# Bank order of the token stages, the third attention's second half and the last stage in a two-layer transformer kernel

## What is computed

```
x = x + g_msa * self_attn(ln(x) * (1 + sc) + sh)             # windows
x = x + g_mca * topk_cross_attn(ln(x) * (1 + sc) + sh, ctx)  # 16 of 154 keys
x = x + g_mlp * (silu(a) * b @ w_m2)                         # SwiGLU
x = x + mha(ln1(x), ln1(x)) + t_sa                           # 1024 keys
x = x + mha(ln3(x), ctx, mask) + t_ca
x = x + gelu(ln2(x) @ w1 + b1) @ w2 + t_mlp
```

## Time and profile before

| | |
|---|---|
| median of 3 runs | 1565.24 us (1562.11 to 1566.72) |
| profiled execution, its own time | 1565.28 us |
| its span in the profile | 1563.5 us |
| mean granted TensorE clock | 0.96 of full |
| PE busy | 1395.5 us, 89% of the span |
| DVE busy | 918.0 us, 59% |
| ACT busy | 716.2 us, 46% |
| POOL busy | 341.6 us, 22% |

### The profile page before, as it was taken

One profiled execution on the slowest core, in us unless ns is written; L12 is line 12 of the kernel. 1 busy time (PEld: TensorE's weight loads), 2 busy tenths in 40 slices (PEclk: granted clock), 3 DMA queues, 4 the chain that ended last, 5 costly groups with the idle time before them and its releaser, 6 DMA issues.

```text
span 1563.5 us, 25438 instructions
## 1 busy us (share of the span) xinstructions
PE 1395.5 (89%) x9100; PEld 681.9 (44%) x9100; DVE 918.0 (59%) x2815; ACT 716.2 (46%) x1454; POOL 341.6 (22%) x377
## 2 busy tenths in 40 slices
PE   7999776879889796889899999999999989987898
PEld 5467554444544452342224333333333334543576
DVE  3556397988877785755465666667576235640220
ACT  2255454555465363115544565555455654543221
...
PEclk9999988789989898989999999999999999999999
...
DMA packets 22092, 26.74 MB, mean 17 GB/s; under 512 B 4204, under 2 KB 19634, under 8 KB 21708
## 3 DMA queue, kind: packets, MB, share of 16 engines
...
...
## 4 chain that ended last, share of the span: by engine, by line
PE 75%; DVE 10%; ACT 6%; issue 5%; POOL 3%; DMA 1%; SPq 0%; ACTq 0%; POOLq 0%; DVEq 0%
PE bank L1022 27%; PE bank L979 10%; PE bank L1062 8%; PE bank L994 7%; PE bank L958 5%; PE bank L937 3%; PE bank L916 2%; PE bank L964 2%; PE bank L1105 1%; DVE x_hat L1441 1%; PE bank L1086 1%; PE bank L944 1%; DVE left L1496 1%; DVE left L1503 1%; ACT pr L1252 1%
## 5 line engine op out<-in xcount | busy, mean ns | idle before, releaser
L1252 ACT ACTIVATE pr<-bank 128x512 f32<-128x512 f32 x656 | 355.0, 597 | 295.8 <-PE bank L1022 291.7
L1468 DVE TENSOR_REDUCE part_max<-bank 128x1 f32<-128x512 f32 x512 | 327.4, 684 | 210.8 <-PE bank L1022 209.8
L1022 PE MATMUL bank<-slot 32*128 32x512 f32 (+1 forms) x3072 | 398.5, 522 | 10.0 <-ACT pr L1252 5.6
L1022 PEld LDWEIGHTS bank<-slot 32*128 32x128 f32 x3072 | 157.6, 185 | 230.5 <-issue 168.6
L1518 POOL TENSOR_SCALAR var_eps<-mean_var 128x4 f32<-128x4 f32 x24 | 5.5, 230 | 966.1 <-DVE mean_var L1432 966.1
L1574 POOL TENSOR_SCALAR left<-left 128x308 f32<-128x308 f32 x128 | 125.2, 978 | 105.0 <-ACT exp_all L1274 45.3
L979 PE MATMUL bank<-h_t,w_m 128*128 128x512 f32 x256 | 130.8, 635 | 11.9 <-ACT hidden L1228 4.7
L1062 PE MATMUL bank<-pr,v 128*17 128x512 f32 x1024 | 135.6, 601 | 0.0
L1576 POOL TENSOR_TENSOR probs<-left,exp_all 128x308 f32<-128x308 f32 x128 | 107.1, 837 | 10.6
L1493 DVE MAX8 top<-bank 128x8 f32<-128x154 f32 x256 | 69.3, 311 | 42.2 <-PE bank L1086 31.9
L1274 ACT ACTIVATE exp_all<-bank,neg 128x154 f32<-128x154 f32 x256 | 85.5, 386 | 10.1 <-DVE left L1496 5.9
...
## 6 DMA issues: line engine op xcount, KB each, us to landing
...
```

What stands on the lines that cost most here:

```text
L1022: last = nc.tensor.matmul(g.bank(*tile)[:, into], left, right, start=True, stop=True)
L1252: nc.scalar.activation(m.pr[:, u % NPR, :], g.bank("s", gi, i)[:, :], ACT.Exp).then_inc(g.free("s", gi, i), 1)
L1468: nc.vector.tensor_reduce(m.part_max[:, slot, h * TB + i // 8, i // 4 % 2:i // 4 % 2 + 1], bank[:, :], axis=AX.X, op=ALU.max).then_inc(don ...
```

## The change

It changes `banks_of`, `own_bank`, the choice of the bank in `finish`, the second half of the third attention in `group_run`, the maxima of group 24 in `last_run`, and where stage (6, 0) lies in `make_plan`.

- In the third attention from round 161 (of -4 to 287) to round 251 the same 364 tiles are written in rounds of four and three in turn: two s and two m, two s and one m, two s and two m, one s and two m. They may take all seven banks, 0 to 6, and so may "o_turn" and "m_turn" of groups 22 and 23, the "s" tiles up to the attention's end, and "on_turn", "y_mm", "hat_turn" and "qk" of stage (5, 0). "pv" of a group of four "s" tiles is written a round later than before. 24 token steps and turns lie in this stretch, as before.
- (2, 1), (3, 0), (4, 0) and the "o_turn" of the second attention take their two banks, 0 and 6, in turn; so does the first half of (3, 1) under the first maxima, and those maxima have banks 1 to 5 left.
- Elsewhere a bank of one's own is taken only if it was last filled more than three steps before.
- The "ug" of stage (6, 0) take the seven banks in turn; its head comes earlier, and its first three "ug" stand between the last "pv" and "o_turn" of the fourth attention.
- The first maxima of group 24 are five rounds of three (one of four) and not four of four.

```diff
@@ -56,6 +57,10 @@
 
 ROUNDS = {1: 4, 3: 32}
 LEAD = {1: 2, 3: 4}
+
+
+THREES = 252 - 7 * 13
+FOURS_AND_THREES = ((2, 2), (2, 1), (2, 2), (1, 2))
 M_HEADS_4 = ((0, 2), (0, 3), (0, 0), (0, 1), (1, 2), (1, 3), (2, 0), (2, 1), (2, 2), (2, 3), (1, 0), (1, 1))
 
 
@@ -79,11 +84,22 @@
 RING = ("o_turn", "on_turn", "y_mm", "hat_turn", "qk", "v", "ua", "ub", "ug", "down", "ck", "cv", "ctx_turn", "mcol", "mgate", "mbv", "mtp")
 
 
+def shares_all(step):
+
+    if step[0] in ("m", "s") and attention(step[1]) == 3:
+        return (step[1] - 16 + (step[0] == "s")) * ROUNDS[3] + step[2] // 2 >= THREES + LEAD[3] * (step[0] == "m")
+    if step[0] in ("m_turn", "o_turn"):
+        return 22 <= step[1] < 24
+    return step[0] in ("on_turn", "y_mm", "hat_turn", "qk") and step[1:3] == (5, 0)
+
+
 def banks_of(step):
 
     kind = step[0]
+    if shares_all(step):
+        return (0, 1, 2, 3, 4, 5, 6)
     if kind in ("m", "m_turn", "s"):
-        return (3, 4, 5, 6) if attention(step[1]) == 1 else (1, 2, 3, 4, 5, 6)
+        return (3, 4, 5, 6) if attention(step[1]) == 1 else (1, 2, 3, 4, 5) if kind == "m" and step[1] == 16 else (1, 2, 3, 4, 5, 6)
     if kind == "c_score":
         return (1, 2, 3, 4)
     if kind == "c_turn":
@@ -101,13 +117,24 @@
     s, b = step[1:3]
     if s == 6:
         return (0, 1, 2, 3, 4, 5, 6)
-    early = (s, b) == (3, 1) and (kind == "ua" and step[3:] == (0, 0) or kind == "hat_turn" and step[3] == 0 or kind in ("on_turn", "y_mm") and step[3] < 2)
-    return (0, 6) if early or (s, b) in ((2, 1), (3, 0), (4, 0)) else (0, 1, 2)
+    return (0, 6) if (s, b) in ((2, 1), (3, 0), (4, 0)) or first_maxima(step) else (0, 1, 2)
+
+
+def first_maxima(step):
+
+    kind, (s, b) = step[0], step[1:3]
+    if (s, b) != (3, 1):
+        return False
+    return step[3] == 0 if kind in ("hat_turn", "ua", "ub") else step[3] < 2
 
 
 def own_bank(step):
 
-    return attention(step[1]) > 1 if step[0] == "o_turn" else step[1:3] in ((2, 1), (3, 0), (4, 0), (3, 1), (4, 1), (5, 0), (5, 1), (6, 0))
+    if step[0] == "o_turn":
+        return 16 <= step[1] < 22 or step[1] >= 24
+    if step[1:3] == (6, 0):
+        return step[0] in ("on_turn", "y_mm", "hat_turn")
+    return step[1:3] in ((4, 1), (5, 1)) or step[1:3] == (3, 1) and not first_maxima(step)
 
 
 SOON = ("ck_a", "cv_copy", "x_hat", "on_copy", "modulate", "ua_copy", "silu", "qk_a", "v_copy")
@@ -163,7 +190,8 @@
             if banks:
                 banks = [x for x in banks if x not in last or last[x][0] != "down_part" or ("down",) + last[x][1:4] in placed]
                 empty = [x for x in banks if x not in last or follow_up(last[x]) in placed]
-                first = banks[0] if step[0] in RING and own_bank(step) and banks[0] in empty else None
+                apart = len(self.steps) - turn.get(banks[0], -9) > 3
+                first = banks[0] if step[0] in RING and own_bank(step) and banks[0] in empty and apart else None
                 bank = min(empty or banks, key=lambda x: turn.get(x, -1)) if first is None else first
                 if not empty:
                     follow = follow_up(last[bank])
@@ -327,6 +355,15 @@
     def time(c):
         return start + first * (min(c, turn) + lead) + then * max(c - turn, 0)
 
+    def round_of(t, width, tiles, double=False):
+        if tiles:
+            plan.at(t, *tiles, ("scores", *tiles))
+        plan.at(t + 0.3 * width, *[("m_red",) + x[1:] for x in tiles if x[0] == "m"], *[("exp",) + x[1:] for x in tiles if x[0] == "s"])
+        for x in tiles:
+            last_of[x] = len(begins) + double
+        begins.append(t)
+
+    begins, last_of, stream = [], {}, ([], [])
     for c in range(-lead, 9 * rounds):
         t, width = time(c), time(c + 1) - time(c)
         gs, xs = c // rounds - 1, c % rounds
@@ -338,27 +375,43 @@
             maxima = [("m", gi_m, i) for i in range(2 * xm, 2 * xm + 4)] if xm % 2 == 0 else []
         if gm > 7:
             weighed = [("s", gi_s, i) for i in range(2 * xs, 2 * xs + 4)] if xs % 2 == 0 else []
-        tiles = [x for both in zip(weighed, maxima) for x in both] if len(weighed) == len(maxima) else maxima + weighed
-        if tiles:
-            plan.at(t, *tiles, ("scores", *tiles))
-        plan.at(t + 0.3 * width, *[("m_red",) + x[1:] for x in maxima], *[("exp",) + x[1:] for x in weighed])
+        if a == 3 and THREES <= c < 8 * rounds - lead:
+            stream[0].extend(weighed)
+            stream[1].extend(maxima)
+            while len(stream[0]) + len(stream[1]) >= 7:
+                k = len(begins) - first_three
+                for j in range(2):
+                    n_s, n_m = FOURS_AND_THREES[(k + j) % 4]
+                    tiles = [x for pair in itertools.zip_longest(stream[0][:n_s], stream[1][:n_m]) for x in pair if x]
+                    del stream[0][:n_s], stream[1][:n_m]
+                    round_of(time(THREES + (k + j) * 0.875), width, tiles)
+        else:
+            tiles = [x for both in zip(weighed, maxima) for x in both] if len(weighed) == len(maxima) else maxima + weighed
+            round_of(t, width, tiles, not (weighed and maxima))
+            first_three = len(begins)
         if c % 2:
             gaps[c] = t + 0.6 * width
-        if gm < 8 and xm == rounds - 1:
-            if a == 3:
-                plan.at(t + 0.5 * width, ("m_neg", gi_m))
-                plan.at(time(c + 1) + 0.35 * (time(c + 2) - time(c + 1)), ("m_turn", gi_m), ("m_copy", gi_m), ("max_rows", gi_m))
-            else:
-                plan.at(t + 0.9 * width, ("m_turn", gi_m), ("m_copy", gi_m), ("max_rows", gi_m))
-        if gs >= 0 and xs % per == per - 1:
-            d = xs // per
-            t1, width = time(c + 1), time(c + 2) - time(c + 1)
-            plan.at(t1 + 0.4 * width, ("pv", gi_s, d))
+    assert not stream[0] and not stream[1]
+    for gi in range((a - 1) * 8, a * 8):
+        c = last_of["m", gi, M_UNITS[a] - 1]
+        t, width = begins[c], begins[c + 1] - begins[c]
+        if a == 3:
+            plan.at(t + 0.5 * width, ("m_neg", gi))
+            plan.at(t + 1.35 * width, ("m_turn", gi), ("m_copy", gi), ("max_rows", gi))
+        else:
+            plan.at(t + 0.9 * width, ("m_turn", gi), ("m_copy", gi), ("max_rows", gi))
+        for d in range(PV_STEPS[a]):
+            c = last_of["s", gi, (d + 1) * S_UNITS[a] // PV_STEPS[a] - 1]
+            c += 2 if a == 3 and begins[c] >= time(THREES) and begins[c] < time(8 * rounds - lead) else 1
+            last = c + 1 >= len(begins)
+            t1 = begins[c] if c < len(begins) else begins[-1] + (c + 1 - len(begins)) * then
+            width = then if last else begins[c + 1] - begins[c]
+            plan.at(t1 + 0.4 * width, ("pv", gi, d))
             if (d + 1) % (PV_STEPS[a] // 2) == 0:
                 half = (d + 1) // (PV_STEPS[a] // 2) - 1
-                plan.at(t1 + 0.9 * width, ("o_copy", gi_s, half))
-                plan.at(t1 + 1.5 * width, ("o_turn", gi_s, half))
-                plan.at(t1 + 1.9 * width, ("o_norm", gi_s, half))
+                plan.at(t1 + 0.9 * width, ("o_copy", gi, half))
+                plan.at(t1 + 1.5 * width, ("o_turn", gi, half))
+                plan.at(t1 + 1.9 * width, ("o_norm", gi, half))
     return time(9 * rounds), gaps
 
 
@@ -382,9 +435,9 @@
         plan.at(t + 0.52 * per, ("o_turn", gi, half))
         plan.at(t + 0.6 * per, ("o_norm", gi, half))
 
-    for x, (gi, numbers) in enumerate(((24, (0, 1, 2, 3)), (24, (6, 7, 8, 9)), (24, (4, 5, 10, 11)), (25, (0, 1, 2, 3)))):
+    for x, (gi, numbers) in enumerate(((24, (0, 1, 2)), (24, (6, 8, 3)), (24, (7, 9, 4)), (24, (5, 10, 11)), (25, (0, 1, 2, 3)))):
         scores(early[x], *maxima_in(gi, *numbers))
-    plan.at(early[3] + 0.3 * per, ("m_turn", 24), ("m_copy", 24), ("max_rows", 24))
+    plan.at(early[3] + 0.6 * per, ("m_turn", 24), ("m_copy", 24), ("max_rows", 24))
     for n in range(16):
         gi, half, t = 24 + n // 2, n % 2, start + n * per
         tails, one, two = [("s", gi, 5 * half)], [("s", gi, 5 * half + i) for i in (1, 2)], [("s", gi, 5 * half + i) for i in (3, 4)]
@@ -526,16 +579,17 @@
     plan.at(where[-1] + 0.1, ("load_row", 8), ("load_out", 6))
     R4 = 6.4
     A4 = end + 0.6 * R4
-    end, gaps4 = last_run(plan, A4, R4, [gaps[c] + 0.1 for c in (267, 271, 275, 279)])
+    end, gaps4 = last_run(plan, A4, R4, [gaps[c] + 0.1 for c in (259, 263, 267, 271, 275)])
     five = joined([gap_slots(5, 1, n) for n in range(2)])
     plan.fill(five, [gaps[c] for c in range(277, 288, 2)] + gaps4[:10])
     plan.at(A4 + 7 * R4, ("load_row", 9), ("load_out", 7))
     six = [[block_slots(6, b, n) for n in range(2)] for b in range(2)]
-    plan.fill(six[0][0][0], gaps4[20:31])
-    for (b0, n0), t in (((0, 1), 19), ((1, 0), 49), ((1, 1), 86)):
+    for b0, n0, t in ((0, 0, 0), (0, 1, 19), (1, 0, 49), (1, 1, 86)):
         six[b0][n0][0].append([six[b0][n0][1][0].pop(0) for _ in range(CK)])
-        plan.spread(six[b0][n0][0], end + t, end + t + 16)
```

(5 more changed lines are left out.)

1 line of the change is left out of this document (added).

## The result

The changed kernel took **1521.0 us** (median of 4 runs, 1520.14 to 1521.69) against 1566.0 for the kernel before (4 runs beside it); the ratio is 0.9717, with a 95% interval of 0.9699 to 0.9735. Forecast were 1515 and a range of 1500 to 1543. The medians and ratios of this document leave out three executions that took far longer: one of 3190.8 and one of 3023.6 us, of the first two kernels under the experiments, and one of 1667.1 us of the kernel before. The kernel before took 1563.1 to 1566.0 us beside the different kernels, so small differences between kernels are better read from the ratios. The profiled execution has a span of 1519.4 us against 1563.5, so 44.1 us are to be found. The page first: busy time, share of the span, instructions, and the granted clock in 40 slices.

The account below looks back on a forecast made before the run. PE's queue, busy 89% of the span, was taken to set the end; waits removed, -18 - 19 - 3 - 6 - 2 - 2 = -50, took 1565.3 to 1515 us, range 1500 to 1543.

Parts of the forecast that it names:

- Last stage: Stage (6, 0): "ug" every 1.72 us instead of 2.76; -18 us, bounds -19 and -14 if the head's x_hat is late.
- Third attention, second half: Rounds of four and three on seven banks end PE's bank waits; -19 us, bounds 0 and -27.
- token steps: Third attention's second half: idle 1.54 and 0.69 before "on_turn" go with own banks; -3 us, bounds 0 and -4.
- 3.38 a period against 3.98; over 45 periods 27 us: Third attention's second half: average period after against before, a full gain of 27 us, of which 70% was taken.
- B's wait: Third attention before: half of a period's second round of four tiles waits 0.85 us for a bank.
- The discount of 30%: Third attention's second half: 70% of 27 us taken, for DVE's bursts and 24 token steps and turns sharing the seven banks.
- First maxima: Taking banks 0 and 6 in turn ends most of about 8.5 us idle; -6 us, bounds +1 and -9.
- Second attention: Banks 0 and 6 alternate, order stays; DVE's lateness makes the step behind wait again; -2 us, bounds +2 and -8.
- Group 23 and fourth attention: With group 24's maxima: seventh bank, second "on_turn" or "hat_turn" on another bank; -2 us, bounds +2 and -6.
- Rival 1: Third attention: two tiles of one head in a round cost a turn, losing 22 us; 1537 us, chance 0.12.
- Rival 2: Third attention: ring of weights (eight "exp" slots) or DVE's bursts bind instead of banks; gain 3 of 22, 1534 us, chance 0.13.
- Rival 3: Third attention: a round costs the same whatever it holds, 1.5 us each; slower, 1579 us, chance 0.05.

Follow-up runs that it names:

- the first two kernels under the experiments: Changed kernel with the second attention's token steps and o_turn on their own bank as before, 1517.3 us; kernel before with only "ug" taking its banks in turn, 1547.9 us.
- its mend: Changed kernel with "o_turn" of groups 20 and 21 also on any of seven banks, not held to bank 0: 1516.2 us.
- extra tiles took the room in B: Kernel before, two score tiles computed twice in 43 second rounds (B) of groups 20 to 22, ahead of B's two tiles that wait for a bank: 1578.6 us.

## Why the prediction was right, and where it was not

**Last stage, -18 forecast, -15.4 measured.** The mechanism and the two cadences (2.76 to 1.72) held, and the bank alone carries it. The head's lateness, for which the bound of -14 stood, took 1.8 of it.

**Third attention, second half, -19; -5.2 measured, and token steps -3; -4.6 measured.** The kernel with this part undone splits the -9.8 of groups 20 to 22 in this way. The first of the two is the step that failed. "3.38 a period against 3.98; over 45 periods 27 us" was right for the tiles: 2.91, 4.33 and 4.84 came nearly as forecast, and without what the periods with a step have over bare ones the stretch falls by 25.0 us (204.2 - 15.2 = 189.0 with the part undone, 199.0 - 35.0 = 164.0 with it). But 3.98 was taken as the price of every period, and the steps in between at nothing changed. At least twelve periods held a step in B's wait, so their 0.85 was spent already; taking the wait away made the step dear. The discount of 30% was laid to DVE's bursts and to steps that shorten a bank's turn; of these, DVE's bursts cost 1.0 us in one bare period. The steps' excess grew by 19.8 us (15.2 to 35.0). Of this 4.8 are "o_turn" on bank 0, by its mend; 10.6 is what lost cover cost when extra tiles took the room in B; the remaining 4.4 stay open. The waits before a second "on_turn" went as the working said, and the bank 0 of "o_turn" put others in their place, though the bound "they meet a bank that a tile just filled" had named that very thing.

**First maxima, -6; -10.5 measured, -8.2 in nine other profiles.** Sized somewhat low. The waits of 0.78 to 1.06 for "ua" and "ub" went, as did those of "hat_turn" behind the first and of the second "on_turn". The 3.18 for "o_norm" stayed: "o_turn" takes bank 0, the "ua" behind it bank 6, and with two banks in turn the next "ua" is back on 0.

**Second attention, -2; +4.4 measured**, past the bound of +2. Of this 1.2 lies ahead of the stage, where the two kernels are the same; over all profiles the banks in turn cost 4.5. "The step behind them in the queue waits again" was the right mechanism, but a wait was priced by its length alone: "down" waits 3.08 and 3.09, and at each such wait the granted clock falls to half, which the sum had not reckoned with. Giving bank 0 back ends both; no run changed the length of the wait alone.

**Groups 16 to 19, nothing forecast; -6.3 measured.** An omission: the rule on bank 0 most likely acts there as well, on "v" and "hat_turn"; it was not run alone. **Group 23 and fourth attention, -2; -6.5 measured**: half a microsecond past the bound of -6, with 4.6 of it in group 23. The time as a whole came near the forecast by some luck: the excess of the small terms made up for a part of the large one.

**The rivals.** Rival 1, a turn for each doubled head, is excluded by the trace of after. Nine bare periods of seven tiles have a round with two tiles of one head: four of four-three take 2.91 like the five without, five of three-four take 2.92 or 3.13 where seven without take 2.91. So a doubled head costs 0 to 0.22 us and not 0.86. The Trainium skill's rule ("TensorE: Matmul & The Clock Gate", Part 3), that matmuls start and end in strict program order, would make each cost a turn; here the measurement decides, and it fits a tile on a free row group going ahead of a neighbour's second pass. Rival 2, a wait under another name, is half true: what the third attention's part gave (5.2 where rival 2 said 3) is near to it, but the ring of weights bound no bare period and DVE's bursts bound one; the wait that did come is for the most part "o_turn" on bank 0. Rival 3 is excluded: four and three tiles take 1.93 us together, not 3.0.
